# A fused attention and FFN kernel: gate and up two steps behind attention, down three, and the weight preparation spread over two steps

## The chip, the cores and the metric

The kernel runs on one core of one Trainium2 chip. The metric is the device time of one launch in microseconds; before and after are compared as medians of several runs. A profile is one execution of the program, so its span differs a little from the median.

## The reference

x is 16 sequences of 512 tokens with 256 features, in float32. Two residual blocks follow each other:

```
x = x + linear_attention(layernorm(x)) @ Wo + bo        # 16 heads of 64
    q, k = relu(x Wq) + 0.001, relu(x Wk) + 0.001 ; v = x Wv
    context = running sum over tokens of k v^T ; attn = q context / (q . running sum of k)
x = x + down( silu(gate(n)) * up(n) ),  n = layernorm(x) # 256 -> 704 -> 256
    every fp4 linear rounds its input and its weight to an FP4 grid
    in blocks of 16 along the contracted axis: scale = max|block| / 6, q = grid(x / scale) * scale
```

## The kernel before, in words

A **chunk** is 128 tokens; a sequence has four (c = 0 to 3), and there are 64 chunks (g = 4 b + c). A **half** is two chunks; LayerNorm 1 and the projections to Q and K are done for a whole half. All five engines run one long unrolled program each, written by hand: `run_steps(step)` calls `step(b, c)` in the same order on each engine, and only semaphores tie them together. Each engine executes its own list strictly in the order written. Matrix products are made of two float32r parts: `..._hi` is ScalarE's copy of the transposed tile, `..._lo` is what is left, VectorE's subtraction (`low`), so each product is three sets of matmuls, hi hi, hi lo and lo hi.

One step of TensorE has, in this order: `turn_x` of the next half (c even), `scores` of chunk g, `turn_k` (c < 3), `project_v` for the next half, `attend` (state part and causal part), `update_state`, `turn_xq` of chunk g-1, `turn_hq` of chunk g-2, `gate_up` of g-1 in two halves with `turn_attn` of g between them, `down` of g-2, `project_out` of g. On odd steps `project_qk` of the next half goes into it in two parts. VectorE masks the scores, normalizes, rounds xn2 and the hidden tile to the FP4 grid (`round_begin`, `round_scale`, `round_end`), and adds the residuals. ScalarE evacuates PSUM and makes the `_hi` parts. GpSimd adds the epsilon to Q and K (`add_eps`), computes rstd with a power, and makes `xq` and `hq` (the scaled grid values). After the last chunk two more steps run only the FFN parts that are left.

**PSUM banks** are given in a fixed turn over a list of keys (`keys`, `bank_of`), eight banks around. `Banks.take` makes TensorE wait for the reader of whatever had that bank last.

**The FFN weights** are prepared on the chip, once, as eight jobs (`ffn_jobs`): gate 0 to 2, up 0 to 2 (512 columns each), down 0 and 1 (704 columns). For each job SP loads a stage tile (`load_ffn_weight`, three stages in turn), VectorE runs `quantize(job)`, seven operations that end with the grid number tile `w_magic`; GpSimd's `round_weights` adds and subtracts that tile and writes the scaled result to `hq`; TensorE turns it (`turn_weights`), ScalarE and VectorE take the high and low part from the bank (`high_ffn_weights`, `low_ffn_weights`). `JOBS_AT` says at which place of which step a job is turned. A job's rounding waits until the job before it is turned, since `hq` is one tile. The jobs 0 and 1 are turned ahead of step 0, then 2 and 3 behind `attend` of step 0, 4 and 5 at its end, 6 and 7 in step 1.

Of the kernel before, what the change touches and what calls it, by code (L numbers as in the profile page):

```python
# [58 lines left out]
def build_program(nc, x, Wq, Wk, Wv, Wo, bo, w_gate, w_up, w_down, out):  # L59
# [25 lines left out]
    with ExitStack() as ctx:  # L85
# [130 lines left out]
        for c in range(CHUNKS):  # L216
            odd, update = c % 2 == 1, c < CHUNKS - 1
            keys += [("x", c, 0)] * (not odd) + [("scores", c, n) for n in range(4)]
            keys += [("k", c, n) for n in range(2) if update]
            keys += [("v", c, n) for n in range(2)] + [("av", c, n) for n in range(4)]  # L220
            keys += [("kv", c, n) for n in range(2) if update] + [("xq", c, 0)] * (not odd)
            for n in range(2):
                keys += [("qk", c, 2 * n), ("qk", c, 2 * n + 1)] * odd + [("xq", c, 0)] * (odd and n == 0)
                keys += [("hq", c, n)]
# [22 lines left out]
        def probs_slot(head):  # L247
# [9 lines left out]
        JOBS_AT = {"before": (0, 1), (0, "attend"): (2, 3), (0, "end"): (4, 5), (1, "attend"): (6,),  # L257
                   (1, "update"): (7,)}
# [9 lines left out]
        w_stage = [hid[:], silu[:].rearrange("p h f -> p (h f)"), h_scaled[:]]  # L268

# [22 lines left out]
        def flat_slots(t):  # L292
# [7 lines left out]
            (as_rows(k_tok[:], 4), wo_hi[:, 4:8, :], wo_lo[:, 4:8, :]),  # L300
# [5 lines left out]
        def _(sp):  # L306
# [50 lines left out]
            def step(b, c):  # L357
# [3 lines left out]
                if exists(g - 2, ALL_CHUNKS):  # L361
                    sp.wait_ge(out_ready, g - 1)
                    sp.dma_start(out_chunks[g - 2], out_sb[:, c % 2, :]).then_inc(out_stored[c % 2], 16)
# [7 lines left out]
        def _(pe):  # L371
# [138 lines left out]
            def turn_xq(b, c, g):  # L510
                pe.wait_ge(xq_ready, g + 1)
                k = banks.take(pe, ("xq", c, 0), b, xqT_ready, lambda b: CHUNKS * b + c)
# [4 lines left out]
            def gate_up(b, c, g, half):  # L517
                cols = slice(half * FH, (half + 1) * FH)
                pe.wait_ge(xqT_hi_ready, g + 1)
                for s, (w_hi, w_lo, done, used) in enumerate(((wg_hi, wg_lo, gate_done, silu_ready),  # L520
                                                              (wu_hi, wu_lo, up_done, hid_ready))):
                    k = banks.take(pe, ("gate_up", c, 2 * half + s), b, used,
                                   lambda b: 2 * (CHUNKS * b + c - 1) + half + 1)
# [7 lines left out]
            def turn_hq(b, c, g, n):  # L531
                pe.wait_ge(hq_ready, g + 1)
                k = banks.take(pe, ("hq", c, n), b, hqT_ready, lambda b: 2 * (CHUNKS * b + c - 2) + n + 1)
# [5 lines left out]
            def down(b, c, g):  # L539
                k = banks.take(pe, ("down", c, 0), b, out_ready, lambda b: CHUNKS * b + c - 1)  # L540
# [30 lines left out]
            pe.wait_ge(wo_w_ready, 2)  # L571
            turn_weights(JOBS_AT["before"])

            def step(b, c):
                g, u = CHUNKS * b + c, UNITS * b + c // 2
                now, before, before2 = (exists(g - n, ALL_CHUNKS) for n in range(3))
                following = exists(u + 1, ALL_HALVES)
                if c % 2 == 0 and following:
# [9 lines left out]
                project = c % 2 == 1 and now and following  # L588
# [559 lines left out]
```

## Time and profile before

| what | value |
|---|---|
| median of 3 runs | 1738.57 us (1734.92 to 1738.92) |
| the profiled execution: its own time | 1739.14 us |
| its span | 1737.3 us |
| TensorE busy | 1676.3 us (96%) |
| VectorE busy | 1167.2 us (67%) |
| ScalarE busy | 650.4 us (37%) |
| GpSimd busy | 463.9 us (27%) |
| mean granted TensorE clock | 0.984 |

The span lies 1.8 us below the time of the same execution. Busy times are sums over the whole span and say nothing of where an engine stood still; the start, the repeating middle and the end have to be looked at one by one.

### The profile page before, as it was taken

What the parts mean: (1) busy time and instruction counts of PE and PEld (TensorE: products, weight loads), DVE (VectorE), ACT (ScalarE), POOL (GpSimd) and SP (SyncE); (2) the same over time, 40 slices, a digit from 0 to 9 for tenths busy, and PEclk for the clock granted to TensorE, in tenths of its full rate; (3) what the DMA queues carried; (4) which work ended last, traced back from release to release, by engine and by line L of the source; (5) the groups of instructions that cost most, each with busy time, mean ns of one, the idle gap of its engine ahead of it and who ended that gap; (6) DMA issues with size and microseconds to landing.
All of it is one profiled execution on the core that took longest, in us unless ns stands there. A gap on an engine that the chain in (4) does not pass through costs nothing.

```text
span 1737.3 us, 46951 instructions
## 1 busy us (share of the span) xinstructions
PE 1676.3 (96%) x20388; PEld 1587.4 (91%) x20388; DVE 1167.2 (67%) x2458; ACT 650.4 (37%) x1233; POOL 463.9 (27%) x643
## 2 busy tenths in 40 slices
PE   5699999999999999999999999999999999999986
PEld 4589999999999999999999999999999999999985
DVE  5866667666666766666766666766666676666674
ACT  4143333343333333333334333334333333433321
POOL 5532212223222222222222222222321222222210
PEclk9899999999999999999999999999999999999996
DMA  3100000000000000000000000000000000000000
GB/s 135 34 2 13 11 14 14 14 5 14 14 11 14 14 5 14 14 11 14 14 14 5 14 11 14 14 13 5 14 14 11 14 14 5 14 14 11 8 8 9
DMA packets 21962, 26.26 MB, mean 15 GB/s; under 512 B 1792, under 2 KB 20736, under 8 KB 21760
## 3 DMA queue, kind: packets, MB, share of 16 engines
q1 hardware_dynamic: 21760, 23.27, 4.1%
q8 instruction: 163, 2.67, 0.6%
q14 instruction: 39, 0.32, 0.1%
HBM read 14.88 MB, written 8.39 MB: 13 GB/s over the span
## 4 chain that ended last, share of the span: by engine, by line
PE 94%; DVE 3%; issue 1%; POOL 1%; ACT 0%; DMA 0%; POOLq 0%; ACTq 0%; DVEq 0%
PE bank L377 63%; PE bank L433 7%; PE bank L473 7%; PE bank L497 3%; PE bank L464 3%; PE bank L443 3%; PE bank L487 3%; PE bank L536 2%; PE bank L514 1%; PE bank L387 1%; DVE probs L999 1%; PE bank L567 0%; DVE w_magic L918 0%; DVE h_amax L950 0%; DMA x_in<-in_L_attn_x 0%
## 5 line engine op out<-in xcount | busy, mean ns | idle before, releaser
L806 POOL TENSOR_SCALAR qkT<-qkT 128x512 f32<-128x512 f32 x256 | 183.8, 722 | 345.8 <-ACT qkT L634 345.8
L634 ACT ACTIVATE qkT<-bank 128x512 f32<-128x512 f32 x256 | 153.1, 598 | 296.4 <-PE bank L377 296.4
L377 PE MATMUL bank<-xT_hi,wqk_hi 128*128 128x256 f32 x1024 | 211.6, 288 | 0.4 <-DVE wd_lo L870 0.4
L377 PE MATMUL bank<-xT_lo,wqk_hi 128*128 128x256 f32 x1024 | 203.2, 279 | 0.0
L377 PE MATMUL bank<-xT_hi,wqk_lo 128*128 128x256 f32 x1024 | 203.1, 279 | 0.0
L825 POOL TENSOR_TENSOR rstd<-var,minus_half 128x1 f32<-128x1 f32 x64 | 35.0, 547 | 517.9 <-DVE var L1051 517.9
L999 DVE TENSOR_TENSOR probs<-bank,causal 128x512 f32<-128x512 f32 x256 | 164.3, 683 | 12.7 <-PE bank L433 12.1
L377 PEld LDWEIGHTS bank<-xT_hi,wqk_hi 128*128 128x128 f32 x1024 | 155.3, 188 | 2.7 <-DVE wd_lo L870 0.6
L377 PEld LDWEIGHTS bank<-xT_lo,wqk_hi 128*128 128x128 f32 x1024 | 156.1, 188 | 0.0
L377 PEld LDWEIGHTS bank<-xT_hi,wqk_lo 128*128 128x128 f32 x1024 | 155.9, 188 | 0.0
L433 PE MATMUL bank<-qkT 64*128 64x128 f32 x2048 | 134.2, 282 | 3.1 <-issue 1.2
L433 PEld LDWEIGHTS bank<-qkT 64*128 64x128 f32 x2048 | 122.3, 191 | 13.7 <-issue 9.4
L473 PE MATMUL bank<-v,probs 128*64 128x65 f32 x4096 | 133.6, 223 | 1.0 <-DVE probs L999 1.0
L870 DVE TENSOR_TENSOR attnT_lo<-bank,attnT_hi 128x512 fp32r<-128x512 f32 x128 | 88.4, 692 | 68.5 <-ACT attnT_hi L681 68.5
L473 PEld LDWEIGHTS bank<-v,probs 128*64 128x64 f32 x4096 | 124.8, 137 | 10.2 <-issue 5.5
L1090 DVE TENSOR_TENSOR hid<-silu,bank 128x352 f32<-128x352 f32 x128 | 66.7, 521 | 89.6 <-PE bank L377 85.7
L870 DVE TENSOR_TENSOR hqT_lo<-bank,hqT_hi 128x512 fp32r<-128x512 f32 (+1 forms) x128 | 68.3, 556 | 83.0 <-ACT hqT_hi L687 80.9
L681 ACT ACTIVATE attnT_hi<-bank 128x512 fp32r<-128x512 f32 x128 | 76.4, 598 | 119.0 <-PE bank L497 119.0
L694 ACT ACTIVATE xn<-x,shift,rstd 128x256 f32<-128x256 f32 x64 | 38.5, 602 | 206.0 <-POOL shift L827 206.0
L833 POOL TENSOR_TENSOR xq<-x_scaled,x_scale 128x256 f32<-128x256 f32 x64 | 39.7, 621 | 264.3 <-DVE x_scaled L913 264.3
L783 POOL TENSOR_TENSOR hq<-h_scaled,h_scale 128x704 f32<-128x704 f32 x64 | 89.0, 1390 | 68.3 <-DVE h_scaled L913 68.3
L911 DVE SCALAR_TENSOR_TENSOR h_scaled<-h_square,h_scaled 128x704 f32<-128x704 bf16 x64 | 63.8, 997 | 51.7 <-ACT h_square L740 51.7
(141 smaller groups left out, 3708.1 us busy)
## 6 DMA issues: line engine op xcount, KB each, us to landing
x_in<-in_L_attn_x SPq DMA_DIRECT2D x32, 256.0 KB, 2.7
out<-out_sb SPq DMA_DIRECT2D x64, 128.0 KB, 1.7
probs<-in_L_attn_Wv SPq DMA_DIRECT2D x1, 1024.0 KB, 5.3
qkT<-in_L_attn_Wq SPq DMA_DIRECT2D x1, 1024.0 KB, 7.3
qkT<-in_L_attn_Wk SPq DMA_DIRECT2D x1, 1024.0 KB, 9.4
attn<-in_L_attn_Wo SPq DMA_DIRECT2D x1, 512.0 KB, 9.9
k_tok<-in_L_attn_Wo SPq DMA_DIRECT2D x1, 512.0 KB, 10.9
hid<-in_L_ffn_w_down SPq DMA_DIRECT2D x1, 352.0 KB, 3.0
```

What stands on the lines that cost most here:

```text
L377: at = pe.matmul(dst, lhs_at(kt), rhs_at(kt), start=first and kt == 0, stop=last and kt == k_tiles - 1)
L433: last = pe.matmul(bank[to[odd]][:, k * P:(k + 1) * P], qkT[rows, PAIRS + pair, t * P:(t + 1) * P], qkT[rows, pair, t * P:(t + 1) * P], st ...
L443: last = pe.transpose(turn[k][:, j, :], qkT[:, PAIRS + 4 * n + j, t * P:(t + 1) * P], ident[:])
L473: last = pe.matmul(bank[to[half][odd]][th * DH:th * DH + DH, j * VW:(j + 1) * VW], probs[:, probs_slot(head), th * DH:th * DH + DH], v[:, ...
L634: act.activation(flat(qkT[:, 2 * m:2 * m + 2, :]), bank[bank_of["qk", c, n]][:], ACT.Relu).then_inc(qk_relu, 1)
L681: act.activation(flat(attnT_hi[:, 4 * n:4 * n + 4, :]), flat(turn[bank_of["attn", c, n]][:]), ACT.Copy).then_inc(attnT_hi_ready, 1)
L783: pool.tensor_tensor(blocks(hq[:, 0:FFN], HB), blocks(h_scaled[:], HB), each(h_scale[:], HB), ALU.mult).then_inc(hq_ready, 1)
L806: pool.tensor_scalar(at, at, QK_EPS, 1.0, ALU.add, ALU.mult).then_inc(qk_ready, 1)
L870: dve.tensor_tensor(dst, src, hi.bitcast(F32), ALU.subtract).then_inc(done, 1)
L911: dve.scalar_tensor_tensor(scaled, square, SQUARE_SHIFT, scaled, ALU.add, ALU.add).then_inc(chain, 1)
L999: dve.tensor_tensor(probs[:, 4 * n:4 * n + 4, :], bank[bank_of["scores", c, n]][:].rearrange("p (h t) -> p h t", t=P), causal[:].rearrange ...
L1090: dve.tensor_tensor(hid[:, half * FH:(half + 1) * FH], silu[:, half, :], bank[bank_of["gate_up", c, 2 * half + 1]][:, 0:FH], ALU.mult).the ...
```

## The change

Chunk g's gate and up run in step g+2 instead of g+1, and its down in step g+3 instead of g+2. `turn_xq` moves from behind `update_state` to the place between `turn_k` and `project_v`; its bank moves with it in `keys`. Three steps follow the last chunk instead of two, and in them `turn_hq` stands behind `gate_up` while there is still a gate and up to do. The weight jobs are turned one by one over steps 0 and 1, job 0 alone ahead of step 0; `quantize` alternates between `w_magic` and the still unused `out_sb` as the tile of grid numbers for jobs 0 to 5. GpSimd makes Wo's low halves ahead of the bias, and the second half of Wo is loaded into `x2` instead of `k_tok`. In step 1 GpSimd rounds jobs 4 and 5 ahead of LayerNorm 2's power.

```diff
-            for c in range(2):
+            for c in range(3):
                 step(SEQS, c)
...
-            keys += [("k", c, n) for n in range(2) if update]
+            keys += [("k", c, n) for n in range(2) if update] + [("xq", c, 0)]
...
-        JOBS_AT = {"before": (0, 1), (0, "attend"): (2, 3), (0, "end"): (4, 5), (1, "attend"): (6,),
-                   (1, "update"): (7,)}
+        JOBS_AT = {"before": (0,), (0, "attend"): (1,), (0, "update"): (2,), (0, "end"): (3,), (1, "scores"): (4,),
+                   (1, "attend"): (5,), (1, "project"): (6,), (1, "end"): (7,)}
...
+        w_magics = [w_magic[:], out_sb[:].rearrange("p k d -> p (k d)")]
+
+        def magic_of(job):
+            return w_magics[job % 2 if job < GATE_UP_JOBS else 0][:, 0:ffn_jobs[job][2]]
+
+        def magic_free(job):
+
+            return 2 * job - 2 if job < GATE_UP_JOBS else 2 * job
...
-            (as_rows(k_tok[:], 4), wo_hi[:, 4:8, :], wo_lo[:, 4:8, :]),
+            (as_rows(flat_slots(x2[:]), 4), wo_hi[:, 4:8, :], wo_lo[:, 4:8, :]),
```

TensorE's step:

```diff
                     if c < CHUNKS - 1:
                         turn_k(b, c)
+                turn_weights(jobs_at(g, "scores"))
+                if gated:
+                    turn_xq(b, c, g - 2)
+                if now:
                     if following:
                         project_v(b, c, u + 1, c % 2)
                     attend(b, c, g, u)
                 turn_weights(jobs_at(g, "attend"))
...
-                if before and not project:
-                    turn_xq(b, c, g - 1)
...
-                    if before2:
-                        turn_hq(b, c, g - 2, n)
+                    if downed and (now or not gated):
+                        turn_hq(b, c, g - 3, n)
+                turn_weights(jobs_at(g, "project"))
                 for n in range(2):
-                    if before:
-                        gate_up(b, c, g - 1, n)
+                    if gated:
+                        gate_up(b, c, g - 2, n)
                     if now:
                         turn_attn(b, c, g, n)
+                if downed and gated and not now:
+                    for n in range(2):
+                        turn_hq(b, c, g - 3, n)
...
-                if before2:
-                    down(b, c, g - 2)
+                if downed:
+                    down(b, c, g - 3)
```

ScalarE (`normed`, `gated` and `downed` say that chunk g-1, g-2, g-3 exists):

```diff
-                if before:
+                high_ffn_weights(jobs_at(g, "scores"))
+                if gated:
+                    act.wait_ge(xq_turned, g - 1)
+                    act.activation(flat(xqT_hi[:]), flat(turn[bank_of["xq", c, 0]][:, 0:KD, :]),
+                                   ACT.Copy).then_inc(xqT_hi_ready, 1)
+                if normed:
                     act.wait_ge(x_scaled_ready, g)
```

GpSimd:

```diff
             rstd_1(0)
             rstd_1(1)
+            low_wo(3)
+            low_wo(4)
+            for n in range(3):
                 add_eps(0, n)
-            round_weights(JOBS_AT["before"])
+            round_weights((0,))
+            for n in range(3, PAIRS):
+                add_eps(0, n)
+            round_weights((1, 2))
+            pool.wait_ge(bias_loaded, 16)
+            add_bias(0, 0)
...
+                if g == 0:
+                    round_weights((3,))
+                if g == 1:
+                    round_weights((4, 5))
                 if exists(g - 1, ALL_CHUNKS):
                     pool.wait_ge(ln2_var, g)
...
+                if g == 1:
+                    round_weights((6,))
...
+                if g == 1:
+                    round_weights((7,))
```

VectorE: `quantize` 3 stands behind the masks of step 0, 4 behind `low_attn` there, 5 behind the masks of step 1, 6 and 7 ahead of and behind its `low_attn`; and

```diff
                     round_scale(x_scaled[:], xn2[:], x_inv[:], XB, x_inv_ready, x_scaled_ready, g - 1)
-
-                left_over = before2 and c % 2 == 1
-                if left_over:
-                    round_h(g - 2)
-                if before:
+                low_ffn_weights(jobs_at(g, "scores"))
+                if gated:
+                    low(flat(xqT_lo[:]), flat(turn[bank_of["xq", c, 0]][:, 0:KD, :]), flat(xqT_hi[:]),
+                        xqT_hi_ready, g - 1, xqT_ready)
+
+                if downed and c % 2 == 1 and now:
+                    round_h(g - 3)
+                if normed:
                     round_end(x_scaled[:], x_square[:], x_square_ready, x_round, x_grid_ready, g - 1)
```

## Rows read from the trace of the kernel before

**Rows 1.** The page, its first part: busy time of each engine.

```profile
PE 1676.3 (96%) x20388; PEld 1587.4 (91%) x20388; DVE 1167.2 (67%) x2458; ACT 650.4 (37%) x1233; POOL 463.9 (27%) x643
```

**Rows 2.** Windows: stretch and its length, busy us (instructions) by engine, clock, DMA.

```profile
33.00:100.00 67.00, 41.37 (x475) 35.59 (x476) 48.83 (x87) 14.99 (x29) 36.01 (x32) 0.80 0.09 27
217.00:1659.00 1442.00, 1440.22 (x17777) 1368.01 (x17776) 975.63 (x2077) 553.23 (x1061) 369.99 (x529) 1.00 0.04 12
1705.50:1737.30 31.80, 15.22 (x76) 14.15 (x75) 13.70 (x29) 4.86 (x10) 4.12 (x5) 0.65 0.04 12
```

**Rows 3.** Waits of TensorE, 30 to 114 us: total, times, longest.

```profile
PE bank L567 <- DVE attn L1033: 6.2, 1, 6.2
```

**Rows 4.** Chain of work, in order of time: start us, us, what.

```profile
219.97 1.03 PE bank L443 x8
...
238.60 1.99 PE bank L433 x32
240.59 3.00 PE bank L377 x12
243.59 1.09 PE bank L464 x64
```

**Rows 5.** Timeline of three engines in an odd step: start us, us, engine.

```profile
240.76 1.88 DVE L999 TENSOR_TENSOR probs<-bank,causal 128x512 f32<-128x512 f32 x3
...
247.09 1.39 POOL L783 TENSOR_TENSOR hq<-h_scaled,h_scale 128x704 f32<-128x704 f32 x1
...
249.76 0.60 PE L536 MATMUL bank<-ident,hq 128*128 128x128 f32 x4
```

**Rows 6.** Timeline of VectorE, one quantize of a 512-wide job.

```profile
47.48 0.68 DVE L950 TENSOR_REDUCE h_amax<-hid 128x32 f32<-128x512 f32 x1
48.19 0.18 DVE L956 TENSOR_SCALAR w_scale<-h_amax 128x32 f32<-128x32 f32 x1
...
50.06 0.43 DVE L921 TENSOR_SCALAR w_magic<-w_magic 128x512 f32<-128x512 f32 x1
```

**Rows 7.** Timeline of GpSimd, rounding of weight jobs.

```profile
43.02 1.27 POOL L793 TENSOR_TENSOR h_scaled<-h_scaled,w_magic 128x512 f32<-128x512 f32 x1 [0.82 <-DVE w_magic L921]
...
45.72 1.06 POOL L800 TENSOR_TENSOR hq<-h_scaled,h_scale 128x512 f32<-128x512 f32 x1
...
78.72 1.71 POOL L795 TENSOR_TENSOR hid<-hid,w_magic 128x704 f32<-128x704 f32 x1
```

**Rows 8.** Timeline of ScalarE and TensorE in the start.

```profile
32.80 1.08 ACT L657 ACTIVATE xn<-x_in,shift,rstd 128x256 f32<-128x256 f32 x2
...
51.94 2.09 PE L473 MATMUL bank<-v,probs 128*64 128x65 f32 x64 [1.01 <-DVE probs L999]
```

**Rows 9.** Windows: one stretch of the start; the clock stands behind POOL.

```profile
88.00:92.00 4.00, 2.11 (x18) 1.75 (x20) 2.82 (x7) 1.83 (x4) 0.45 (x1) 0.50 0.00 0
```

**Rows 10.** Timeline of TensorE, the first transpose of step 2.

```profile
114.10 0.60 PE L387 MATMUL bank<-ident,xn 128*128 128x128 f32 x4
```

**Rows 11.** Timeline of VectorE, an operation on 44 columns.

```profile
78.82 1.66 DVE L956 TENSOR_SCALAR w_scale<-h_amax 128x44 f32<-128x44 f32 x1
```

**Rows 12.** Timeline of TensorE in the tail.

```profile
1715.44 0.94 PE L377 MATMUL bank<-wg_hi,xqT_hi 128*128 128x352 f32 x2
...
1720.84 0.86 PE L377 MATMUL bank<-wd_hi,hqT_hi 128*128 128x256 f32 x6
...
1722.24 0.86 PE L377 MATMUL bank<-wd_hi,hqT_lo 128*128 128x256 f32 x6
```

**Rows 13.** Timeline of VectorE and GpSimd in the tail.

```profile
1707.42 0.41 DVE L1118 TENSOR_TENSOR x<-bank,x_bias 128x256 f32<-128x256 f32 x1
...
1713.14 0.62 POOL L833 TENSOR_TENSOR xq<-x_scaled,x_scale 128x256 f32<-128x256 f32 x1 [3.49 <-DVE x_scaled L913]
...
1721.59 0.89 DVE L897 TENSOR_REDUCE h_amax<-hid 128x44 f32<-128x704 f32 x1
...
1726.84 1.39 POOL L783 TENSOR_TENSOR hq<-h_scaled,h_scale 128x704 f32<-128x704 f32 x1 [13.08 <-DVE h_scaled L913]
```

More of the change, by code:

```diff
@@ L539, in down @@
             def down(b, c, g):
-                k = banks.take(pe, ("down", c, 0), b, out_ready, lambda b: CHUNKS * b + c - 1)
+                k = banks.take(pe, ("down", c, 0), b, out_ready, lambda b: CHUNKS * b + c - 2)
                 dst = bank[k][:, 0:DIM]
@@ L575, in step @@
                 g, u = CHUNKS * b + c, UNITS * b + c // 2
-                now, before, before2 = (exists(g - n, ALL_CHUNKS) for n in range(3))
+                now, gated, downed = exists(g, ALL_CHUNKS), exists(g - 2, ALL_CHUNKS), exists(g - 3, ALL_CHUNKS)
                 following = exists(u + 1, ALL_HALVES)
+                project = c % 2 == 1 and now and following
                 if c % 2 == 0 and following:
@@ L675, in step @@
                 g, u = CHUNKS * b + c, UNITS * b + c // 2
-                now, before, before2 = (exists(g - n, ALL_CHUNKS) for n in range(3))
+                now, normed = exists(g, ALL_CHUNKS), exists(g - 1, ALL_CHUNKS)
+                gated, downed = exists(g - 2, ALL_CHUNKS), exists(g - 3, ALL_CHUNKS)
                 following = exists(u + 1, ALL_HALVES)
+                project = c % 2 == 1 and now and following
                 def high_attn(n):
@@ L734, in step @@
                         high_attn(half)
+                if downed and gated and not now:
+                    for n in range(2):
+                        high_hq(n)
                 if project:
@@ L1041, in step @@
                     low_x(c, u + 1)
-                if before:
+                if normed:
                     dve.wait_ge(ln2_stats, g)
@@ L1076, in step @@
                     add_state()
[L1077 to L1081 removed]
                 low_ffn_weights(jobs_at(g, "update"))
[L1083 removed]
+                if downed and (now or not gated):
                     for n in range(2):
                         low_hq(n)
+                if is_step(1):
+                    quantize(6)
+                low_ffn_weights(jobs_at(g, "project"))
                 for half in range(2):
[L1087 to L1089 removed]
+                    if gated:
+                        dve.wait_ge(up_done, 2 * (g - 2) + half + 1)
+                        dve.wait_ge(silu_ready, 2 * (g - 2) + half + 1)
                         dve.tensor_tensor(hid[:, half * FH:(half + 1) * FH], silu[:, half, :],
@@ L1094, in step @@
                         low_attn(half)
+                if downed and gated and not now:
+                    for n in range(2):
+                        low_hq(n)
                 if is_step(0):
-                    quantize(6)
-                if before:
-                    round_begin(h_amax[:], h_scale[:], h_inv[:], hid[:], hid_ready, 2 * g, h_amax_ready,
-                                h_scale_ready, h_inv_ready, g - 1)
-                    round_scale(h_scaled[:], hid[:], h_inv[:], HB, h_inv_ready, h_scaled_ready, g - 1)
+                    quantize(4)
+                if is_step(1):
+                    quantize(7)
+                if gated:
+                    round_begin(h_amax[:], h_scale[:], h_inv[:], hid[:], hid_ready, 2 * (g - 1), h_amax_ready,
+                                h_scale_ready, h_inv_ready, g - 2)
+                    round_scale(h_scaled[:], hid[:], h_inv[:], HB, h_inv_ready, h_scaled_ready, g - 2)
                 if norm:
```

136 lines of the change are left out of this document (54 added, 82 removed).

## The prediction

> **What bounds the kernel now.** I read the page first: TensorE is busy 96% of the span [rows 1]. The windows then say where the other 4% is [rows 2]: between 217 and 1659 us TensorE works 1440.2 of 1442.0 us, while from 33 to 100 us it works 41.4 of 67 us and in the last 31.8 us only 15.2. So for some 60 of 64 chunks the kernel is a queue of matrix work with nothing to take out by another order, and the change removes no matmul. It can earn or lose at the two ends only, unless it makes a stall in the middle. The list of TensorE's waits in the start shows what the idle 26 us are made of [rows 3]: it stands before the weight transposes (L567), once for 6.2 us, because VectorE and GpSimd are late with a weight job and everything else is queued behind it.
>
> **The change in the middle.** Every step has the same matmuls and the same vector work, moved by one chunk. Three things could break it. (a) The bank table moves: at c=3 the third and fourth attention banks are now those of the last two score banks (0 and 1), so `attend` starts only after the last causal mask. In the trace the masks of such a step end at 240.76 + 1.88 = 242.6, and attend began at 243.6 [rows 4, 5]; xq's turn, now ahead of it, adds 0.3 of slack. No cost. (b) VectorE does xqT_lo (0.4) ahead of rounding h on odd steps, so hq comes 0.4 later. It was ready at 247.09 + 1.39 = 248.5 and turned at 249.8 [rows 5]; of 1.3, some 0.6 is left, as TensorE comes there 0.3 earlier too. No cost. (c) turn_xq stands between scores and v at c=3: one more change of shape on TensorE, at most 0.1 each in 16 steps. I take +0.5; below, 0, above, 2. The chain xn2 to xq, which gets a whole step more, was not waited for in the middle, so that slack earns nothing there.
>
> **The start, step by step.** Durations: one quantize on VectorE is 47.48 to 50.49 = 3.0 us [rows 6]; one rounding of a 512-wide job on GpSimd is 43.02 to 46.78 = 3.75; with 704 columns it starts with 1.7 for 1.3 [rows 7], from which I estimate 4.9 there and 3.7 on VectorE. On TensorE at full clock scores are 2.0, turn_k 1.0, project_v 2.8 to 3.0, attend 2.0, plus 1.1 where there is a state [rows 4, 8].
> Until 33.9 us (the second half's normalized x [rows 8]) nothing moves: job 0 is rounded between the eps steps by 30.3 and turned at 32.3, beside work that was there. Step 0: transposes 0.7, scores, turn_k, v, attend bring TensorE to 42.4; before, it got there at 54.0 [rows 8], since two jobs were rounded ahead of it. This is the gain. Then a ladder: w1 turned 43.0 (quantized at 37.3), its low half 44.4 frees bank 6 for the state update (45.4), the state add 46.1 frees bank 7 for w2 (46.8), whose low half (48.0) frees bank 7 for the second attention transpose (48.6). VectorE ends low_attn at 50.0, quantizes job 4 (53.0), adds x2 (53.9), and ends low w3 at 54.6 and the masks of step 1 at 57.3. TensorE has finished project_out (2.85) at 52.2, w3 52.9, scores and turn_k 55.9, and turns w4, rounded by 56.7, until 57.5.
> Step 1: quantize(5) 60.4; GpSimd now has round_weights((4, 5)) ahead of LayerNorm 2, so job 5 ends at 64.2, shift at 65.0, ScalarE's xn2 at 65.65, and behind it in ScalarE's order two k_tok copies and the high half of w4, 67.3. VectorE's low w4 stands behind round_scale and ends at 68.0. Its bank, 1, is that of project_v. So **TensorE waits from 57.5 to 68.0**, 10.5 us, in a place where it waits for nothing now. Then v 4.6 (half clock), attend 3.1, w5 and update 77.4, first four groups of Q and K (5.6) 83.2. quantize(6), behind the state add, ends 81.9, GpSimd 86.9: a wait of 3.7. w6 and the attention transposes 89.2, the other groups 94.8, project_out 97.4. quantize(7) ends 94.9, LayerNorm 1 96.2; GpSimd does rstd_1, the last two eps, then job 7: 103.3. A wait of 5.9. w7 turned 104.8, and the scores of step 2 wait for its low half (banks 5 and 6): 106.2.
> Clock: from 88 to 92 us, behind the wait of 6.2, it was 0.50, which is the 1.2 GHz level [rows 3, 9]; so the waits of 10.5 and 5.9 us are each followed by work at half speed. I put about 1.8 us into project_v and 0.6 into the scores of step 2, inside the sum.
> Before, turn_x of step 2 began at 114.10 and its scores, 2.0 long, at 114.7 [rows 10]. At the end of those scores the new kernel is at 108.8 against 116.7: **-7.9**. Bounds: every wait clean and the clock up, -11; clock down from 43 on as well (project_out at half speed, +2.3) and contention on each quantize, -2.
> On contention: an operation on 44 columns, 0.18 at 48.2, took 1.66 while GpSimd worked, and ended with GpSimd's instruction (78.72 + 1.71) [rows 6, 7, 11]. In the walk above quantize(5), (6) and (7) run with GpSimd idle or on short eps steps, so I add nothing for them; the upper bound has 1.5 each.
> The Trainium skill (SBUF — State Buffer, Who interferes with whom) has it that the port pair that VectorE shares with GpSimd is an exclusive lock, held for the whole instruction. The trace agrees, with 1.66 for 0.18. By it, packing both engines' weight work tighter costs the loser one GpSimd instruction each time, and the start would give some 3 to 4 us less; the rows lead to the same bound.
>
> **Work shifted out of the middle.** Step 2 no longer has hq and down of chunk 0. Turning hq is 0.6, down 2.2 (1720.84 to 1723.1) [rows 12]: **-2.8** for everything behind. It comes back in the tail, with one more gate and up.
>
> **The tail.** In clock times of the trace of before: step 63 still waits for hq, now chunk 60's, at the same place in GpSimd's order, 0.4 later: x2(63) at 1707.8. Before, from x2 at 1707.4 the line went xq(63) at 1713.8, gate and up from 1715.4 to 1720.8, rounding from 1721.6 to hq at 1728.2 (6.6), then turn, down and store until 1737.3 (9.1) [rows 12, 13]. Now step 64 has chunk 62's gate and up. Its high half sits on ScalarE behind xn2 of chunk 63, so it starts only at 1711.2, at half clock, ends 1716.9; hq(61) and down(61) until 1720.9. xq(63), ready since 1714.6, is turned at 1721.3, but its high copy sits behind h_square(62) (1722.8) and its low half on VectorE behind rounding h(62) and out(61) (1725.1). Gate and up end 1728.4; low_hq(62), put ahead of rounding h(63), ends 1730.6; 6.6 and 9.1 more: 1746.3. **+9.0**. Bounds: +2 if only chunk 62's gate and up (4.3 to 5.4) got in the way and half of it hid behind the xn2 to xq chain; +13 if the last gate and up ran at half clock.
>
> **Sum.** 1737.3 - 7.9 - 2.8 + 0.5 + 9.0 = 1736.1 of span, 1737.9 with the 1.8 around it. That execution (1739.1) is 0.6 above the median of 1738.57; less those 0.6, I say 1737.3. A difference below 0.3% (5.2 us) can't be told from none here.
>
> **The rivals.**
> 1. *Same (forecast, 0.54).* What the start gives is paid back in the tail: 1737.3, own range 1733.5 to 1743.5.
> 2. *Faster (0.26).* The tail hides most of the added chunk: three chunks overlap there, and TensorE has 16.6 idle us in the last 31.8 [rows 2]. With the tail at +2: 1730.5. Against it: in-order ScalarE and VectorE queues put chunk 62 ahead of chunk 63 four times.
> 3. *Slower (0.14): the start gives nothing.* The new waits in step 1 are long chains over three engines. If the walk is short by more than 8 us there (each quantize stretched by 1.5, GpSimd's job 7 behind the eps steps), scores of step 2 come at 114 and the sum is 1745.5. It decides from 112 us on.
> 4. *Slower (0.06): a stall in every odd step.* The slack of hq is 0.6; if hq came 0.9 later it would cost 0.3 in 31 steps, 9 us: 1747. Against it, 1.3 us between hq and its turn [rows 5].
> Faster 0.26, same 0.54, slower 0.20. The range, 1729 to 1747, goes from the tail at its lower bound to rival 4.
>
> **What the changed profile would show.** Right: TensorE still idle about 1% or less from 217 us on; a wait of 9 to 12 us before project_v of step 1, whose last link is VectorE's low w4, and one of 4 to 7 before w7's transposes; scores of step 2 at 104 to 109; from the last x2 to the end 37 to 40 us instead of 30. Wrong if step 1's wait is under 5 us or the tail under 34 us (faster), if scores of step 2 come after 112, or if `probs` or hq appear among TensorE's waits in the middle (slower).

## The result, and the profile after

| | before | after |
|---|---|---|
| median | 1738.74 us, 6 runs (1734.92 to 1739.46) | 1744.5 us, 6 runs (1743.21 to 1745.42) |
| ratio, 95% interval | 1 | 1.0036 [1.0024, 1.0049] |
| span of the profiled execution | 1737.3 | 1743.4 |

The change made the kernel 0.36% slower by the ratio, and the interval excludes 1. I had said 1737.3 and no difference that can be told. The time lies inside the range of 1729 to 1747, but on the other side of before, and that it lies inside is luck: the middle gave 4.2 us that I had not seen coming, and without them it would be 1748.7. The page has the same engine in front, the same instructions, and a little less work on VectorE and GpSimd than in [rows 1]:

```profile
PE 1678.0 (96%) x20388; PEld 1590.3 (91%) x20388; DVE 1159.6 (67%) x2458; ACT 647.5 (37%) x1233; POOL 454.8 (26%) x643
```

The windows of start, middle and tail answer to [rows 2]; the middle begins 2 us sooner here and the tail ends with the longer span:

```profile
33.00:100.00 67.00, 46.79 (x519) 41.63 (x520) 39.28 (x80) 16.40 (x31) 32.87 (x32) 0.80 0.10 30
215.00:1659.00 1444.00, 1443.85 (x17841) 1373.60 (x17840) 975.66 (x2086) 551.12 (x1062) 363.58 (x530) 1.00 0.04 12
1705.50:1743.40 37.90, 22.22 (x116) 20.13 (x115) 14.86 (x27) 6.43 (x13) 3.40 (x3) 0.81 0.03 10
```

Two things stand in them. In the middle TensorE's idle time fell from 1.8 us of 1442.0 to 0.15 of 1444.0. In the tail TensorE now works 22.2 us where it worked 15.2, in a stretch that is 6.1 us longer.

To place the difference I read off the timeline when the scores of a step begin:

| scores of step | before | after | offset |
|---|---|---|---|
| 0 | 44.15 | 33.69 | -10.5 |
| 1 | 72.88 | 58.00 | -14.9 |
| 2, begin | 114.63 | 112.44 | -2.2 |
| 2, end | 116.7 | 116.0 | **-0.7** |
| 3 | 135.25 | 132.80 | **-2.45** |
| 63 | 1682.52 | 1675.84 | **-6.7** |
| the end of the span | 1737.3 | 1743.4 | **+6.1** |

Read downwards, the bold ones and the steps between them give the four terms: start -0.7, work shifted out of the middle -1.75, middle -4.2, tail +12.8; their sum is +6.1. The forecast had -7.9, -2.8, +0.5 and +9.0, sum -1.2.

How far one profile carries is read from the other kernels' profiles with the same code in a stretch. From step 3 to step 63 the eight other kernels that keep the changed bank table all took 1542.6 to 1543.0 us, so the middle is sure to some tenths. Scores of step 3 began between 132.77 and 133.08 in the four profiles with this start (after, e4, e7, e12), so start and shift together, -2.45, are sure as well; how they split is not, as the scores of step 2 began anywhere from 111.28 to 112.44. The tail, from the scores of step 63 to the end, was 66.2 to 68.0 in five profiles with the changed code (after, e2, e5, e6, e9) and 54.8 and 52.8 in two with the old (before, e11): the +12.8 could be 11.4 or 15.2.

**The start** gained 14.9 us by step 1 and then lost nearly all of it. TensorE's waits from 30 to 114 us (total, times, longest) name the places; the one of [rows 3] is gone:

```profile
PE bank L387 <- DVE wu_lo L896: 11.3, 2, 11.1
PE bank L577 <- POOL hq L815: 9.0, 2, 5.6
PE bank L497 <- DVE wg_lo L896: 3.0, 1, 3.0
```

The first is project_v of step 1, which needs the bank of job 4's transposes. The chain of work ahead of it (start us, us, what) shows what that bank waits for. VectorE's `low` of job 4 (`wu_lo`) takes 0.70 us, but it stands behind job 5's rounding on GpSimd and all of LayerNorm 2:

```profile
65.16 1.26 POOL h_scaled L808
...
66.50 1.27 POOL h_scaled L810
...
67.84 1.06 POOL hq L815
68.90 0.53 POOL rstd L850
...
69.72 0.60 ACT xn L710
70.32 0.97 ACT k_tok L715 x2
71.29 0.50 ACT wu_hi L666
...
71.81 0.70 DVE wu_lo L896
```

**The tail.** TensorE's waits from 1660 us on:

```profile
PE bank L546 <- POOL hq L798: 7.8, 2, 4.9
PE bank L387 <- ACT xqT_hi L720: 4.7, 1, 4.7
PE bank L524 <- DVE out_sb L1142: 3.4, 1, 3.4
```

The second I had foreseen (the high half of xq(62) behind xn2 of chunk 63), the third not. The timeline around it:

```profile
1713.36 0.79 ACT L755 ACTIVATE h_square<-h_scaled 128x704 bf16<-128x704 f32 x1 [3.22 <-DVE h_scaled L932]
1714.18 0.89 DVE L937 SCALAR_TENSOR_TENSOR h_scaled<-h_square,h_scaled 128x704 f32<-128x704 bf16 x1 [0.85 <-ACT h_square L755]
1715.11 0.89 DVE L939 SCALAR_TENSOR_TENSOR h_scaled<-h_square,h_scaled 128x704 f32<-128x704 bf16 x1
1715.92 0.42 DVE L1142 TENSOR_TENSOR out_sb<-bank,x 128x256 f32<-128x256 f32 x1
...
1716.48 0.63 PE L524 MATMUL bank<-ident,xq 128*128 128x128 f32 x2 [3.43 <-DVE out_sb L1142]
```

xq(63) is turned into bank 0, which `down` of chunk 61 had last. The add that reads it takes 0.42 us and stands on VectorE behind the rounding of h(62), which waits for ScalarE's square. `down(61)` was done at 1713.05.

### The profile page after: what moved, and what is told of

It is laid out like the page before. It is cut to its first block, busy times and chain, and to the rows that moved or that the text cites. A ratio compares the mean times of both kernels' runs of the same rounds, so it can differ in the third digit from the quotient of the medians.

```text
span 1743.4 us, 47014 instructions
## 1 busy us (share of the span) xinstructions
PE 1678.0 (96%) x20388; PEld 1590.3 (91%) x20388; DVE 1159.6 (67%) x2458; ACT 647.5 (37%) x1233; POOL 454.8 (26%) x643
## 4 chain that ended last, share of the span: by engine, by line
PE 92%; DVE 4%; POOL 1%; ACT 1%; issue 1%; DMA 0%; POOLq 0%; DVEq 0%
PE bank L387 62%; PE bank L483 7%; PE bank L443 7%; PE bank L507 3%; PE bank L474 3%; PE bank L546 3%; PE bank L453 3%; PE bank L497 3%; PE bank L524 1%; PE bank L397 1%; DVE probs L1022 0%; PE bank L577 0%; DVE hid L988 0%; DVE h_amax L976 0%; DVE w_magic L944 0%
## 5 line engine op out<-in xcount | busy, mean ns | idle before, releaser
L821 POOL TENSOR_SCALAR qkT<-qkT 128x512 f32<-128x512 f32 x256 | 174.9, 689 | 322.7 <-ACT qkT L649 322.7
L1022 DVE TENSOR_TENSOR probs<-bank,causal 128x512 f32<-128x512 f32 x256 | 163.9, 682 | 10.9 <-PE bank L443 10.5
L443 PEld LDWEIGHTS bank<-qkT 64*128 64x128 f32 x2048 | 120.9, 190 | 11.1 <-issue 6.1
L937 DVE SCALAR_TENSOR_TENSOR h_scaled<-h_square,h_scaled 128x704 f32<-128x704 bf16 x64 | 69.9, 1092 | 51.8 <-ACT h_square L755 51.8
```

What stands on the lines that cost most here:

```text
L443: last = pe.matmul(bank[to[odd]][:, k * P:(k + 1) * P], qkT[rows, PAIRS + pair, t * P:(t + 1) * P], qkT[rows, pair, t * P:(t + 1) * P], st ...
L821: pool.tensor_scalar(at, at, QK_EPS, 1.0, ALU.add, ALU.mult).then_inc(qk_ready, 1)
L937: dve.scalar_tensor_tensor(scaled, square, SQUARE_SHIFT, scaled, ALU.add, ALU.add).then_inc(chain, 1)
L1022: dve.tensor_tensor(probs[:, 4 * n:4 * n + 4, :], bank[bank_of["scores", c, n]][:].rearrange("p (h t) -> p h t", t=P), causal[:].rearrange ...
```

## The experiments

Twelve kernels ran. Each expectation names two theories, A and B, with what each would show. "After" is the changed kernel; every diff is against it if nothing else is said, and every ratio is to the kernel before. The other half of the change alone, the new weight schedule at the old depth, was not tried: job 7 has `silu` as its stage tile, and gate_up(0) would write `silu` in step 1.

**e2_depth_only: the new depth with the old weight schedule.**

```diff
-        JOBS_AT = {"before": (0,), (0, "attend"): (1,), (0, "update"): (2,), (0, "end"): (3,), (1, "scores"): (4,),
-                   (1, "attend"): (5,), (1, "project"): (6,), (1, "end"): (7,)}
+        JOBS_AT = {"before": (0, 1), (0, "attend"): (2, 3), (0, "end"): (4, 5), (1, "attend"): (6,),
+                   (1, "update"): (7,)}
...
-            return w_magics[job % 2 if job < GATE_UP_JOBS else 0][:, 0:ffn_jobs[job][2]]
+            return w_magic[:, 0:ffn_jobs[job][2]]
```

> The depth of the changed kernel with the weight preparation of before (jobs 0 and 1 ahead of step 0, 2 to 5 in step 0, 6 and 7 in step 1, one tile of grid numbers). Theory A (the new weight schedule gives nothing in the start, because step 1 stands still for job 4): with the old schedule the scores of step 2 begin at 109 to 111 us, earlier than the 112.4 of the changed kernel, and the time is 1739 to 1743, that is 1 to 5 us under the changed kernel. Theory B (the new schedule is what made the start as early as it is, and the loss is all in the tail): scores of step 2 later than 114, time 1746 or more.

Measured: 1741.2 us, ratio 1.0017 [1.0008, 1.0026]; scores of step 2 at 110.45, of step 3 at 129.30, of step 63 at 1672.16. The old schedule reaches step 2 two us sooner than the new one and step 3 3.5 us sooner. Theory A: with the depth fixed, spreading the weights earned nothing and costs 3.3 us. That the old schedule does better here than in the kernel before (114.63) I put down to the depth, which takes gate_up(0) out of step 1; no run shows that by itself.

**e5_ln2_first: GpSimd does LayerNorm 2 of step 1 between jobs 4 and 5.**

```diff
-                    round_weights((4, 5))
+                    round_weights((4,))
...
+                    if g == 1:
+                        round_weights((5,))
```

> The changed kernel with LayerNorm 2's two GpSimd instructions of step 1 ahead of the rounding of weight job 5 instead of behind it. Theory A (TensorE's 11.1 us before project_v of step 1 hang on the chain job 5, shift, xn2, round_scale, low half of w4): the wait falls to 5 to 6 us, scores of step 2 begin 5 us earlier, 1739 to 1740. Theory B (something behind it in step 1, job 5 to job 7 on GpSimd, takes it up again): the wait falls, scores of step 2 move by less than 2 us, 1743 to 1744.

Measured: 1740.54 us, 1.0018 [1.0008, 1.0027]. The wait of 11.1 fell to 7.3 (5 to 6 expected), the scores of step 2 began at 106.71 (-5.7), of step 3 at 128.34 (-4.5). Theory A, with a longer rest of the wait.

**e6_w4_first: the high and low half of job 4 ahead of LayerNorm 2 on ScalarE and VectorE.** On ScalarE:

```diff
-                if normed:
+                if normed and g != 1:
...
+                if g == 1:
+                    act.wait_ge(ln2_shift, g)
+                    act.activation(xn2[:], x2[:, (c - 1) % CHUNKS, :], ACT.Identity, bias=shift2[:],
+                                   scale=rstd2[:]).then_inc(xn2_ready, 1)
```

and on VectorE `low_ffn_weights(jobs_at(g, "scores"))` moves up ahead of `quantize(5)`.

> The changed kernel, in step 1 only: ScalarE copies k_tok and the high half of job 4 ahead of xn2, and VectorE takes job 4's low half ahead of quantize(5). GpSimd's order is as changed, so the chain to xn2 is as long as before. Theory A (the bank of job 4 alone holds project_v): the wait of 11.1 us falls to 2 to 3 us; the transposes of job 5 then wait for v's copies, which stand behind xn2 on ScalarE, and the scores of step 2 come 5 to 7 us earlier, 1738 to 1740. Theory B (all of step 1 hangs on xn2, not on the bank): the wait moves to another place and the scores of step 2 move by under 2 us, 1743.

Measured: 1739.05 us, 1.0003 [0.9994, 1.0013]. The scores of step 2 began at 105.33, of step 3 at 127.06. The wait shrank to 1.6, and one of 4.9 came up behind it:

```profile
PE bank L577 <- POOL hq L819: 7.7, 2, 4.4
PE bank L577 <- ACT v L642: 4.9, 1, 4.9
PE bank L387 <- DVE wu_lo L900: 1.6, 1, 1.6
```

ScalarE now takes v out of its banks behind xn2, and job 5's transposes want those banks. Even so this order alone gives back 5.5 us of the 5.8 that the change lost.

**e9_warm: matmuls of no use in the wait before project_v of step 1.**

```diff
+                if g == 1:
+                    pe.wait_ge(probs_ready, 8)
+                    for i in range(30):
+                        pe.matmul(bank[bank_of["v", 1, 1]][:], xT_hi[:, i % KD, 0:P],
+                                  wv_hi[:, i % KD, 0:512], start=True, stop=True)
```

> The changed kernel with 30 more matmuls of 512 columns (their result is overwritten) in the 11 us that TensorE waits ahead of project_v in step 1, so that project_v, the reads of the state and the values of that step run at the full clock instead of half. Theory A (half clock is part of the lost start): project_v there takes about 2.9 us instead of 5.4, the scores of step 2 start 2 to 3 us earlier (near 110 instead of 112.4) and the time falls by 2 to 3 us, to 1742. Theory B (the chain of weight jobs 6 and 7 sets the start of step 2, TensorE only waits): project_v is as short, but the waits in front of the turns of jobs 6 and 7 grow by the same amount, the scores of step 2 stay within 0.5 us of 112.4 and the time stays at 1744.5.

Measured: 1742.56 us, 1.0027 [1.0017, 1.0038]; the interval overlaps that of after, so the time says little. The trace says more. The scores of step 2 began 2.4 us sooner, as A has it, but 1.6 of that was there before the added matmuls: project_v began at 71.06 instead of 72.65, as the scores of step 1 began at 56.34 instead of 58.00. In this profile project_out of step 0, the same code, ran at the full clock and took 2.9 us (52.87 to 55.81), where it took 5.3 in after; what it saved arrived at project_v almost whole:

```profile
52.87 1.19 PE L387 MATMUL bank<-wo_hi,attnT_hi 128*128 128x256 f32 x8 [0.78 <-ACT attnT_hi L702]
53.90 1.11 PE L387 MATMUL bank<-wo_lo,attnT_hi 128*128 128x256 f32 x8
54.85 1.12 PE L387 MATMUL bank<-wo_hi,attnT_lo 128*128 128x256 f32 x8
```

The clock held for the first half of project_v, and was at half again for the second:

```profile
60.70 7.25 PE L600 MATMUL bank<-wv_hi,xT_hi 128*128 128x512 f32 x30
71.06 0.70 PE L387 MATMUL bank<-wv_hi,xT_hi 128*128 128x512 f32 x2 [3.11 <-DVE wu_lo L901]
...
72.55 1.06 PE L387 MATMUL bank<-wv_hi,xT_hi 128*128 128x512 f32 x2
```

project_v took 4.26 us instead of 5.46. The waits before the turns of jobs 6 and 7 were 3.3 and 5.6, against 3.4 and 5.6 in after: they did not grow. So what is gained ahead of them does arrive at step 2, against B.

**e3_xq_back and e3b_xq_back_two: turn_xq back behind update_state, keys too.** The first has the edit alone:

```diff
-            keys += [("k", c, n) for n in range(2) if update] + [("xq", c, 0)]
+            keys += [("k", c, n) for n in range(2) if update] 
...
-                if gated:
-                    turn_xq(b, c, g - 2)
...
+                if gated and not project:
+                    turn_xq(b, c, g - 2)
```

> The changed kernel with xq's transposes, their copies and their bank key back where they stood before (behind update_state, or behind the first Q and K groups), depth and weights as changed. Between the scores of step 3 and of step 63 the changed kernel gained 4.2 us on the one before. Theory A (the place of turn_xq makes it, 0.24 us in each c=3 step): the gain is gone, the stretch is 4 us longer, time 1748 to 1749. Theory B (it comes from the hq and down of another chunk, or from other banks): the stretch stays as it is, time 1744 to 1745.

Measured: 1832.19 us, 1.054 [1.0525, 1.0556]. That is another matter than the one asked: with one xq tile, GpSimd stands before its next write until the last one is turned, now a step late. GpSimd's list of waits:

```profile
POOL xq L865 <- PE bank L525: 482.6, 61, 10.1
```

and TensorE in turn waits 73.3 us for hq, in 32 pieces. e3b has two xq tiles as well.

> As e3_xq_back, but with two xq tiles in turn, so that GpSimd doesn't stand before the write of xq until TensorE has turned the one before late in the step (that wait made e3_xq_back 88 us slower and left its question open). Theory A (the place of turn_xq between scores and v makes the gain of 4.2 us from step 3 to step 63): the stretch takes 4 us more than in the changed kernel, 1748. Theory B (the gain comes from other parts of the new order): stretch as in the changed kernel within 1 us, 1744.

Measured: 1741.93 us, 1.0018 [1.0008, 1.0027]. Step 3 to step 63 took 1547.5 us (129.14 to 1676.63): the kernel before has 1547.3, after 1543.0. The gain of the middle is gone, as theory A had it. The total is lower than expected because the scores of step 3 came 3.7 us sooner and the tail was 3.5 us shorter (64.1 for 67.6); no run says why. But this kernel puts back two things at once, xq's place and the bank table, and the reason that I had given, a cheaper change of shape ahead of project_v, does not stand in the timeline: from the scores of c = 3 to the state matmuls it is 5.16 us in after (132.80 to 137.96) and 4.98 in e3b (129.14 to 134.12). It is longer there with xq, by xq's own 0.19. The difference lies at the end of the step, between the transposes of xn and the scores of c = 0. The kernel before:

```profile
165.33 0.60 PE L387 MATMUL bank<-ident,xn 128*128 128x128 f32 x4
165.53 0.42 DVE L1118 TENSOR_TENSOR x<-bank,x_bias 128x256 f32<-128x256 f32 x1 [1.08 <-PE bank L377]
...
166.03 0.63 PEld L433 LDWEIGHTS bank<-qkT 64*128 64x128 f32 x9 [0.34 <-issue]
166.06 0.68 PE L433 MATMUL bank<-qkT 64*128 64x128 f32 x7
```

The changed kernel:

```profile
162.84 0.60 PE L397 MATMUL bank<-ident,xn 128*128 128x128 f32 x4
163.37 1.27 PE L443 MATMUL bank<-qkT 64*128 64x128 f32 x18
```

From the first transpose to the scores it is 0.73 us and 0.53. Before, the first score bank of c = 0 was the one that `project_out` of c = 3 had last, so it came free with VectorE's x2 add, at 165.53 + 0.42 = 165.95. In the changed table the xq key stands further ahead in each step, and the code that spreads the keys leaves one place empty at c = 1 and one at c = 3. `project_out` of c = 3 so moved two banks on, from 1 to 3, and bank 3 is wanted first by the second group of scores. Nothing in the list of waits shows it; "issue" does not name the add. Two more kernels ask whether it is the bank.

**e11_old_keys_swapped** is the kernel before and **e12_new_keys_swapped** the changed one, each with one edit:

```diff
-            keys += [("x", c, 0)] * (not odd) + [("scores", c, n) for n in range(4)]
+            keys += [("x", c, 0)] * (not odd) + [("scores", c, n) for n in ((2, 1, 0, 3) if c == 0 else range(4))]
```

> The kernel before with two names in the bank table swapped for c = 0 and nothing else: the first group of scores then stands on the bank that turn_attn had last, the second on that of project_out. Theory A (the 4.2 us that the middle gained with the change are a wait for the bank: in the kernel before, the scores of c = 0 wait for VectorE's x2 add, which frees project_out's bank, and the changed table moved that wait away): the 0.2 us between the transposes of xn and the scores go at each of the 15 sequence starts, the stretch from the scores of step 3 to those of step 63 is 3.0 us shorter (1544.3 instead of 1547.3), and the time falls by about 3 us, ratio 0.998. Theory B (the gain is xq's place ahead of project_v, by the cost of a change between shapes of matmul): nothing changes, 1547.3 and a ratio of 1.000.

> The changed kernel with the same two names swapped for c = 0, which puts the first group of scores on project_out's bank, as it was before the change; xq stays ahead of project_v. Theory A (the bank): from the scores of step 3 to those of step 63 it takes 1546.1 us, 3.0 more than the 1543.1 of the changed kernel, and the time rises by about 3 us to 1747.5. Theory B (xq's place): 1543.1 and 1744.5, as the place is kept.

Measured: e11 1733.84 us, ratio 0.9975 [0.9965, 0.9985], step 3 to step 63 1544.3 us (135.10 to 1679.41). e12 1747.36 us, 1.0055 [1.0041, 1.0069], 1546.1 us (132.85 to 1678.96). Both stretches are theory A's to 0.1 us, and theory B's are 3 us off. The rows of the scores from 130 to 1659 us (busy, mean ns, idle before), first the kernel before, then e11, after and e12:

```profile
L433 PE MATMUL bank<-qkT 64*128 64x128 f32 x1888 | 121.3, 278 | 1.9
```

```profile
L433 PE MATMUL bank<-qkT 64*128 64x128 f32 x1888 | 121.3, 278 | 0.0
```

```profile
L443 PE MATMUL bank<-qkT 64*128 64x128 f32 x1920 | 123.3, 278 | 0.0
```

```profile
L443 PE MATMUL bank<-qkT 64*128 64x128 f32 x1888 | 121.3, 278 | 1.9
```

So 3.0 of the middle's 4.2 us are the bank, shown in both directions. The 1.2 that are left seem to go with xq's place, which is argued only: in e3b and e12 the first group stands on the bank that `project_out` had last, and they differ by 1.4, but also in the number of xq tiles and in other banks. e11 is 1.6 us faster than A said; in its profile 2.0 us lie behind the scores of step 63, of which I claim none.

**e4_out_first: in the tail, the output add ahead of the rounding of h.**

```diff
+                if downed and not now:
+                    dve.wait_ge(down_done, g - 2)
...
+                    dve.tensor_tensor(out_sb[:, c % 2, :], bank[bank_of["down", c, 0]][:, 0:DIM],
+                                      x2[:, (c - 3) % CHUNKS, :], ALU.add).then_inc(out_ready, 1)
...
-                if downed:
+                if downed and now:
```

> The changed kernel with VectorE's residual add of the output ahead of rounding h in the three last steps, instead of behind it. The add frees bank 0, for which the transposes of xq of chunk 63 waited 3.4 us. Theory A (that bank is on the path of the tail): 2 to 5 us less, 1740 to 1742. Theory B (the low half of xq, which still stands behind rounding h of chunk 62, sets the same time): under 1 us less, 1744.

Measured: 1742.26 us, 1.0024 [1.0014, 1.0033], 2.2 us below after by the medians; the intervals overlap. TensorE's wait for `out_sb` fell from 3.4 to 0.8, and 1.3 of the 2.6 came back as a longer wait for xqT_lo, 2.3 for 1.0. So the bank itself gave 1.3; gate_up(63) was besides 0.8 us shorter in this profile (5.6 for 6.5), by less of it at half clock. Theory A, at its lower edge.

**e7_tail_order: the tail's queues of ScalarE and VectorE written anew,** chunk 62's gate and up ahead of chunk 63's normalization and rounding, the output add ahead of round_h. ScalarE's part:

```diff
+                if not now:
+                    if gated:
+                        act.wait_ge(xq_turned, g - 1)
+                        act.activation(flat(xqT_hi[:]), flat(turn[bank_of["xq", c, 0]][:, 0:KD, :]),
+                                       ACT.Copy).then_inc(xqT_hi_ready, 1)
+                        for half in range(2):
...
+                    if normed:
+                        act.wait_ge(ln2_shift, g)
```

> The changed kernel with another order in its three last steps: ScalarE takes the high half of xq and both silu of chunk g-2 ahead of xn2 of chunk g-1, VectorE the low half of xq and both products of hid ahead of rounding x, and adds the output ahead of rounding h. Theory A (the tail is 45 us instead of 32 because the queues of ScalarE and VectorE put chunk 62 and chunk 63 behind each other): 8 to 11 us less, 1734 to 1736. Theory B (the tail is as long as it is because of the work of one more chunk, in any order): less than the 2.3 us that e4_out_first gave, 1742 or more.

Measured: 1739.88 us, 1.0007 [0.9998, 1.0017], 4.6 us below after where 8 to 11 were expected; in the profile the tail from the scores of step 63 is 60.3 us, for 67.6 in after and 54.8 before. gate_up(62) starts 4.5 us sooner but waits 1.7 for a bank that the output add holds, and down(61) waits 3.2 for hqT_lo:

```profile
PE bank L546 <- POOL hq L822: 6.3, 2, 4.9
PE bank L387 <- DVE hqT_lo L920: 4.2, 2, 3.2
PE bank L474 <- DVE probs L1046: 1.8, 1, 1.8
PE bank L387 <- DVE out_sb L1201: 1.7, 1, 1.7
```

**e8_start_and_tail: e5, e6 and e7 together.**

> e5_ln2_first, e6_w4_first and e7_tail_order together. If start and tail are separate losses, they add: 7 to 10 us from the start and 8 to 11 from the tail, 1724 to 1729, faster than both kernels. If the start's gain is taken up again by job 7 on GpSimd at the end of step 1, only the tail's is left beside that of e5: 1730 to 1733.

Measured: 1730.61 us, 0.9953 [0.9938, 0.9968]. It beats both kernels, but it is 1.6 us short of the 1724 to 1729 that two separate losses would give, and lies in the 1730 to 1733 of the other case. That case's reason, a start whose gain is taken up again, is not what the trace shows: the scores of step 2 began at 101.56, 10.9 us ahead of after (7 to 10 expected) and 13.1 ahead of the kernel before, and the 4.9 that e6 left is 1.2 with e5 added. What is short is the tail: 64.0 us from the scores of step 63, for 60.3 in e7 with the same code. gate_up(63) alone took 6.6 us here, at half clock for the most part, and 4.1 in e7 (1712.92 to 1717.0), where the window's clock was 1.00.

**e10_warm_tail: e8 with matmuls of no use in three waits of the tail.** Against e8:

```diff
+            def warm(k, hids, count):
+                pe.wait_ge(hid_ready, hids)
+                for i in range(count):
+                    pe.matmul(bank[k][:], xT_hi[:, i % KD, 0:P], wv_hi[:, i % KD, 0:512],
+                              start=True, stop=True)
...
+                if g == 65:
+                    warm(4, 124, 6)
+                if g == 66:
+                    warm(6, 128, 18)
...
+                if g == 64:
+                    warm(4, 124, 14)
```

> The kernel with the new order of the start and of the tail (e8, 1730.6 us) with 6, 14 and 18 more matmuls of 512 columns, whose results nobody reads, in three waits of TensorE behind step 63: ahead of gate_up(63), ahead of down(61), and ahead of the turns of hq(63). Theory A (half clock of the tail is on the path): gate_up(63) takes 4.1 instead of 6.7 us and the turns of hq(63) and down(63) 3.5 instead of 5.8, so the time falls by 3 to 5 us, to 1726 to 1728. Theory B (VectorE and GpSimd set the tail): matmuls get shorter and the waits behind them longer by as much, 1730 to 1731. If the added matmuls last past the end of a wait they cost what they overrun, up to 1 us each.

Measured: 1728.1 us, 0.9941 [0.9923, 0.9958], 2.5 us below e8 by the medians (the intervals overlap; the spans are 1725.8 and 1728.9). gate_up(63) ran from 1703.37 to 1710.0 in e8 and from 1703.47 to 1707.5 here, 2.6 us less. The windows from 1700 to 1710, with the clock behind POOL, first e8:

```profile
1700.00:1710.00 10.00, 7.99 (x30) 7.08 (x28) 3.16 (x6) 2.10 (x4) 1.39 (x1) 0.55 0.04 13
```

then e10:

```profile
1700.00:1710.00 10.00, 6.81 (x40) 5.78 (x39) 4.26 (x8) 2.98 (x6) 1.39 (x1) 1.00 0.04 13
```

That is theory A for gate_up(63), and 2.5 to 3.1 us in all where 3 to 5 were expected. Before down(63) TensorE waited 1.2 us, behind 18 of the added matmuls and the turns of hq(63), and down(63) then ran at half clock (0.51 from 1719.3 to 1722.8), as slow as in e8 (1.64 us for its first six matmuls); only the turns of hq(63) took 0.88 for 1.54. The Trainium skill (TensorE: Matmul & The Clock Gate, Part 1) says that the throttled clock is the default and that activity releases it. The rows of 1.00 against 0.55 agree, and here the activity was matmuls whose results nobody reads.

## Why the prediction was wrong, step by step

The forecast of the span was 7.3 us too low: 7.2 from the start, 1.0 from the shift and 3.8 from the tail, less 4.7 in the middle. The start decided it.

**What bounds the kernel: right but for one wait (see the middle).** TensorE is 96% busy again, and the kernel's matmuls are the same in number.

**The start, -7.9, was -0.7: the walk went wrong in step 0.** I had "TensorE has finished project_out (2.85) at 52.2". It began at 52.02 and lasted to 57.3, at half clock throughout; the timeline answers to the 2.85 with

```profile
52.02 2.05 PE L387 MATMUL bank<-wo_hi,attnT_hi 128*128 128x256 f32 x8 [0.78 <-ACT attnT_hi L697]
53.87 1.91 PE L387 MATMUL bank<-wo_lo,attnT_hi 128*128 128x256 f32 x8
55.58 1.91 PE L387 MATMUL bank<-wo_hi,attnT_lo 128*128 128x256 f32 x8
```

That is 2.4 us, and I had it as a bound only ("project_out at half speed, +2.3"), not in the sum. The other 2.7 came before project_out began, 1.5 of them in the wait of update_state for job 1's low half, which was 2.95 where the ladder had 1.4 (43.0 to 44.4). The scores of step 1 began at 58.0 instead of some 53, and VectorE's job 5, LayerNorm 2 and project_v all hang on that: project_v began at 72.65 for 68.0, 4.7 late. Half clock then cost 0.8 more in project_v (5.4 for 4.6) and 1.0 in the scores of step 2 (3.6 for 2.6); 0.8 lies between the two. That makes the 7.2. The pessimistic bound of -2 was missed too; by its own terms (2.3 for project_out and 1.5 for each of three quantizes) it comes to -1.1. The form of the walk was right: a wait of 11.1 for the 10.5 forecast, released by the low half of job 4, 3.4 for 3.7 before job 6 and 5.6 for 5.9 before job 7. That the place is this chain is shown by e5 and e6, which shorten it and bring the scores of step 2 forward by 5.7 and 7.1 us. That half clock counts is shown for project_v by e9, in 1.2 us, and for project_out by the same profile: there it ran 2.3 us shorter, having begun 0.9 later, and the scores of step 1 and project_v began 1.7 and 1.6 sooner than in after. Rival 3, "the start gives nothing", had the right outcome, and the sign against the forecast that I had named, scores of step 2 after 112, came true at 112.44. Its reason, quantizes stretched by contention, did not: quantize(5) took 62.07 to 65.09, 3.0 us as in [rows 6].

The operation on 44 columns that took 1.66 us [rows 11] took 0.19 in job 6 and 0.60 in job 7:

```profile
97.64 0.60 DVE L982 TENSOR_SCALAR w_scale<-h_amax 128x44 f32<-128x44 f32 x1
```

Over the whole span VectorE was busy 1159.6 us, for 1167.2 before, with the same 2458 operations. By the Trainium skill (SBUF — State Buffer, Who interferes with whom) I had named 3 to 4 us less gain, if both engines' weight work were packed tighter. These operations did not show it; the loss lay elsewhere.

**The shift, -2.8, was -1.75.** The steps moved as said; 0.8 us of it went into a wait of project_out for attnT_hi in step 2, whose cover hq and down had been.

**The middle, +0.5, was -4.2: a wait that I had not seen.** "So for some 60 of 64 chunks the kernel is a queue of matrix work with nothing to take out by another order" rests on 1.8 idle us [rows 2], and those 1.8 were one wait in each sequence, for the x2 add. I looked at the bank table at c = 3 only, where the change looked harmful, and not at c = 0, where it helped. Price: 3.0 us (e11, e12). The bank term (a) and the slack of hq (b) were right: no masks and no hq among the waits. The term for a change of shape (c) had the wrong sign: from xq's first transpose to TensorE's next work it is 0.14 to 0.19 us at the new place and 0.21 to 0.27 at the old one.

**The tail, +9.0, was +12.8: the clock of the last gate and up was in a bound and not in the sum.** Forecast times are in before's clock; 6.7 is taken off them here. gate_up(62) was to start at 1704.5 and end at 1710.2; it ran from 1703.07 to 1708.64, its first half at half clock (0.50 from 1703 to 1705.9). "xq(63), ready since 1714.6, is turned at 1721.3", that is at 1714.6, failed: I had it wait for its own readers and not for its bank, and it was turned at 1716.48, behind the add into `out_sb`. But this cost little against the forecast, which let the low half of xq(63) come late for another reason: it was to be ready at 1718.4 and was at 1717.98. Then the forecast had 3.3 us from there to the end of gate_up(63) and it took 6.6, at half clock until 1723.2 (0.50 in the window). So gate_up(63) ended at 1724.6 for 1721.7, and the rest, rounding, turns, down and store, took 18.8 us for 17.9. The bound of +13, "if the last gate and up ran at half clock", was for just that. e10 shows the clock's price (2.6 us in gate_up(63), against e8), e4 the bank's (1.3), and e7 that the order of the queues costs 4.6 in all by the medians and 7.2 between the two profiles, 2.4 of them in the length of gate_up(63), that is by the clock.

Rival 2, the tail hidden, was wrong in part for the reason named against it, the in-order queues: with them reordered (e7) the tail is still 5.5 us longer than before. Rival 4 did not come up. The profile's sign for the tail, 37 to 40 us from the last x2 to the end, was passed as well: 43.5 (1699.87 to 1743.4).

## What to carry to other kernels

When a key is moved in a rotating bank table, every bank behind it has a new neighbour: print for each key who had the bank last before and after, and ask of each new pair when that reader ends, in the tail above all, where readers are late. In a chain over in-order queues it is the short operation at the end of a long list (a copy of 0.7 us, an add of 0.4) that holds a bank: move it ahead of the long work. Where a forecast walks through waits, the clock behind each wait belongs into the sum and not into a bound. And here the deeper pipeline paid its extra stage at the end, 11 to 15 us of tail; it paid off only with reordered queues (e8, 1730.61 us, and 1728.1 with matmuls of no use added), where the change as made gave 1744.5. No run has the reordered start and tail at the old depth, so it is not shown that the depth earned any of that: with the old weight schedule it made the kernel 0.17% slower (e2), and the swap of two keys alone, at the old depth, 0.25% faster (e11).

## What the runs showed of the hardware

Idle TensorE time of 0.2 us per sequence, with a real wait on a semaphore behind it, stood in the profile as 0.34 us of "issue" ahead of the weight load and in no list of waits; removing it saved 3.0 us of the kernel. The same code met the two levels of TensorE's clock at different places from one profile to the next. Step 0 took 24.3, 23.2, 22.7 and 22.1 us in the profiles of after, e7, e5 and e9, with a granted clock of 0.50, 0.58, 0.67 and 0.86 from 50 to 57 us; gate_up(63) took 4.1 us in e7 and 6.6 in e8, behind waits for xqT_lo of the same 1.4 us. So a difference of one or two us in the start or the tail of one profile is no finding.
